# Moving work across the two joints of a batch in a software-pipelined transformer and expert kernel

## The reference

```python
xn = layernorm(x)                       # 16 x 512 x 128, f32
# branch 1
h = layernorm(xn) * g1 + b1
q, k, v = h@WQ+bQ, h@WK+bK, h@WV+bV     # 16 heads of 8
a = softmax(q k^T / sqrt(8), band: 0 <= i-j < 128)
attn_out = (a v) @ WO + bO
s_t = A * s_(t-1) + (h @ Bw)_t;  ssm_out = s @ Cw
g = sigmoid(h @ Wg + bg)
x1 = xn + g * attn_out + (1 - g) * ssm_out
h2 = layernorm(x1) * g2 + b2
S = x1 + gelu(h2 @ W1 + b1) @ W2 + b2   # the MLP, 128 -> 512 -> 128
# branch 2: 8 experts, top 2, in bf16 inputs
nf = rmsnorm(bf16(xn)) * nw;  w = softmax over the two largest of nf @ gate
out2 = bf16(xn) + sum over e of w_e * expert_e(nf)    # gated, clipped at 7
result = x + S * silu(out2)
```

## Time and profile before

| | |
|---|---|
| median of 3 runs | 1091.38 us (1089.91 to 1097.93) |
| profiled execution, its own time | 1094.57 us |
| its span | 1092.8 us |
| busy: TensorE, VectorE, ScalarE, GpSimd | 84%, 72%, 65%, 46% of the span |
| mean granted TensorE clock | 0.925 |
| DMA, mean | 69 GB/s |

### The profile page before, as it was taken

One profiled execution on the slowest core, in us unless ns is written; L12 is line 12 of the kernel. 1 busy time (PEld: TensorE's weight loads), 2 busy tenths in 40 slices (PEclk: granted clock), 3 DMA queues, 4 the chain that ended last, 5 costly groups with the idle time before them and its releaser, 6 DMA issues.

```text
span 1092.8 us, 38402 instructions
## 1 busy us (share of the span) xinstructions
PE 919.2 (84%) x15864; PEld 561.7 (51%) x15864; DVE 782.5 (72%) x1990; ACT 712.8 (65%) x1126; POOL 501.8 (46%) x786
## 2 busy tenths in 40 slices
PE   2567898989889898988889898989888898978877
PEld 1333564646455464645555464645555464635435
DVE  4476777887877677888777777887777788656216
ACT  3205685858677595858768595867768585746645
POOL 6226355372736356273626456273635547152331
PEclk7557999999999899999999999998999999978869
DMA  5552414123332404224241503223241402310000
GB/s 108 129 118 67 93 46 105 32 94 64 100 62 75 90 27 108 50 90 62 92 75 53 112 24 109 52 90 63 75 93 36 111 17 99 58 31 6 25 1 10
DMA packets 85599, 75.24 MB, mean 69 GB/s; under 512 B 9329, under 2 KB 79154, under 8 KB 85426
## 3 DMA queue, kind: packets, MB, share of 16 engines
q1 hardware_dynamic: 83346, 72.00, 28.3%
q10 hardware_dynamic: 2080, 0.79, 0.3%
HBM read 36.33 MB, written 30.15 MB: 61 GB/s over the span
## 4 chain that ended last, share of the span: by engine, by line
PE 48%; DVE 25%; issue 13%; ACT 9%; POOL 2%; DMA 2%; DVEq 0%; SPq 0%; POOLq 0%; ACTq 0%
PE ps L558 8%; DVE mx L1074 6%; PE ps L500 6%; PE ps L690 5%; PE ps L750 5%; PE ps L711 5%; ACT pt L831 4%; PE ps L489 3%; DVE gc L1131 3%; PE ps L570 2%; DVE lin L1124 2%; PE ps L575 2%; ACT ot L836 2%; DVE junk L950 2%; PE ps L684 2%
## 5 line engine op out<-in xcount | busy, mean ns | idle before, releaser
L831 ACT ACTIVATE pt<-ps 128x1024 f32<-128x1024 f32 (+1 forms) x256 | 234.7, 917 | 212.5 <-PE ps L489 211.1
L1074 DVE TENSOR_REDUCE mx<-ps 128x2 f32<-128x320 f32 (+1 forms) x512 | 230.9, 466 | 110.6 <-PE ps L515 107.6
L1253 POOL TENSOR_SCALAR_AFFINE_SELECT pt<-pt 128x512 f32<-128x512 f32 x256 | 170.7, 669 | 264.6 <-ACT pt L831 264.3
L500 PE MATMUL ps<-kd,qz 48*32 48x160 bf16 (+1 forms) x4096 | 160.5, 241 | 66.6 <-DVE mx L1074 34.2
L489 PE MATMUL ps<-qz,kd 51*32 51x256 bf16 (+1 forms) x4096 | 183.5, 272 | 6.1 <-ACT pt L831 3.8
L558 PE MATMUL ps<-pt,va 128*32 128x256 f32 (+1 forms) x2048 | 159.8, 397 | 33.2 <-ACT ot L836 33.0
L500 PEld LDWEIGHTS ps<-kd,qz 48*32 48x32 bf16 x4096 | 72.7, 91 | 218.7 <-issue 121.3
L690 PEld LDWEIGHTS ps<-m,act_t 128*128 128x128 f32 x1024 | 126.8, 191 | 53.6 <-DVE act_t L1152 38.6
L690 PE MATMUL ps<-m,act_t 128*128 128x128 f32 x1024 | 143.2, 283 | 11.6 <-DVE act_t L1152 11.6
L1256 POOL TENSOR_SCALAR_AFFINE_SELECT pt<-pt 128x512 f32<-128x512 f32 x192 | 124.6, 649 | 0.0
L879 ACT ACTIVATE lin<-ps,mbias 128x512 f32<-128x512 f32 x128 | 87.7, 685 | 48.7 <-DVE act_t L1152 29.5
(11 more groups left out here) (158 smaller groups left out, 1672.7 us busy)
## 6 DMA issues: line engine op xcount, KB each, us to landing
qz<-qk_parts SPq DMA_DIRECT2D x32, 384.0 KB, 7.3
kd<-qk_parts SPq DMA_DIRECT2D x32, 384.0 KB, 8.7
qk_parts<-qp SPq DMA_DIRECT2D x16, 384.0 KB, 2.4
qk_parts<-kp SPq DMA_DIRECT2D x16, 384.0 KB, 2.3
xl<-L_attn_x SPq DMA_DIRECT2D x16, 256.0 KB, 3.1
qk_parts<-qp SPq DMA_DIRECT2D x16, 256.0 KB, 2.9
qk_parts<-kp SPq DMA_DIRECT2D x16, 256.0 KB, 2.7
xnr<-xn SPq DMA_DIRECT2D x16, 256.0 KB, 3.3
```

What stands on the lines that cost most here:

```text
L500: nc.tensor.matmul(ps[QG * c:QG * (c + 1), 4 + par, w * pr:w * (pr + 1)], qz[q][rows, 2 * g + pr, P * i + QG * c:P * i + QG * (c + 1)], kd ...
L831: nc.scalar.activation(to, src, ACT.Exp, scale=SCALE).then_inc(exp_ok.sem, 1)
L1074: nc.vector.tensor_reduce(mx[:, i, HG * g + pr:HG * (g + 1):2], src, AX.X, ALU.max).then_inc(mx_ok.sem, 1)
L1253: sel1 = nc.gpsimd.affine_select(out=pt[:, s, :, 0:P], in_=pt[:, s, :, 0:P], compare_op=ALU.is_ge, fill=0.0, base=0, pattern=[[0, HG], [1, ...
```

## The change

- **Joint 1, TensorE and ScalarE.** `up(0)` with its share is issued in step 16, between the last values, and the two products of `up(1)` in step 17. The share product has a signal of its own (`share_ps`), and is waited for by VectorE's `gate`. ScalarE runs `lin(0)` and `ga(0)` before `aoT`. VectorE makes x1 during experts 1 (before: 0), its statistics during expert 2 (before: 1), and half of the statistics of batch b+3 during expert 0 (before: 2). h2 is made after expert 5 and transposed after `up(7)`.
- **Maxima.** `LEAD = 2`: the scores and maxima of steps 0 and 1 of batch b+2 are done at the end of body b (`first_scores`, `maxima`), and step n of the loop carries those of step n+2. The minus maxima are split and transposed in steps 14 and 15.
- **Joint 2.** The MLP's second product of batch b-1 is done in the next body, half in step 0 and half in step 1 (`mlp_down`); `sres` is made in step 2, the product with the states in step 1 (before: 0). `norm_h`, the two tanh and `finish` move into the steps. `norm_x` moves from ScalarE to VectorE, with four `tensor_scalar` (subtract, multiply) in place of four activations, and GpSimd no longer makes `b1n`. GpSimd's `ob` moves from step 2 to step 5.

The core of the diff:

```diff
-AT_STATES, AT_H0, AT_Q, AT_K, AT_U, AT_V, AT_G, AT_C = 0, 2, 4, 6, 8, 10, 12, 14
+LEAD = 2
+AT_STATES, AT_H0, AT_Q, AT_K, AT_U, AT_V, AT_G, AT_C = 1, 2, 4, 6, 8, 10, 12, 14
-AT_H2 = 4
-MIX = (9, 11, 15, 16)
+AT_H2 = 5
+MIX = (11, 13, 15, 16)
...
+            def maxima_free(b, n, half):
+                if n == 0 and half == 0:
+                    pe.wait_ge(*done(stacks_in, b))
+                    pe.wait_ge(*done(gc_ok, b - 2, E))
+                else:
+                    pe.wait_ge(*done(mx_ok, b, 2 * n - 1 + half))
+
+            def first_scores(b, q, n, half):
+
+                maxima_free(b, n, half)
+                for pr in range(2):
+                    score(b, q, n, half, pr)
+                score_mask(n, half)
...
+                def mlp_down(t):
+                    pe.wait_ge(*done(hid_ok, b - 1))
+                    for j in range(NJ):
+                        mm = nc.tensor.matmul(bank_t(6)[:, t], hid[:, j, P * t:P * (t + 1)], w2[:, j], start=j == 0, stop=j == NJ - 1)
+                    if t == NT - 1:
+                        mm.then_inc(w2_ps.sem, 1)
...
+                    if has(b - 1) and n < 2:
+                        mlp_down(2 * n)
+                        mlp_down(2 * n + 1)
...
+                    if main and n == NCH:
+                        up(0)
+                        share(0)
+                    if main and n == NCH + 1:
+                        up(1)
+                    if nxt and n == NCH - LEAD + 1:
+                        turn_shift()
...
-                    for t in range(NT):
-                        for j in range(NJ):
-                            if t == 0:
-                                pe.wait_ge(*done(hid_ok, b, j + 1))
-                            mm = nc.tensor.matmul(bank_t(6)[:, t], hid[:, j, P * t:P * (t + 1)], w2[:, j], start=j == 0, stop=j == NJ - 1)
-                    mm.then_inc(w2_ps.sem, 1)
...
+                    for n in range(LEAD):
+                        for half in range(2):
+                            first_scores(b + 2, q, n, half)
...
+            def norm_x(b, q, tiles):
+                if tiles[0] == 0:
+                    dve.wait_ge(*done(r1_step, b))
+                    dve.wait_ge(*done(xn_copied, b - 2))
+                for t in tiles:
+                    ts = nc.vector.tensor_scalar(xn[:, q, t], xl[:, q, t], mv[:, t, 0:1], r1[:, t:t + 1], ALU.subtract, ALU.mult)
+                ts.then_inc(xn_ok.sem, 1)
...
+                        if has(b - 1) and step == 5:
+                            dve.wait_ge(*done(w2_ps, b - 1))
+                            dve.wait_ge(*done(x1b_ok, b - 1))
+                            dve.wait_ge(*done(ob_ok, b - 2))
+                            nc.vector.tensor_tensor(sres[:], bank_t(6), x1b[:], ALU.add).then_inc(s_ok.sem, 1)
+                        if has(b - 1) and step in (7, 9):
+                            finish(b - 1, (step - 7) // 2)
...
-                        if e == 0:
+                        if e == 1:
                             dve.wait_ge(*done(wo_ps, b))
...
-                    if n == 2 and has(b - 1):
+                    if n == 5 and has(b - 1):
                         pool.wait_ge(*done(w_ok, b - 1))
```

More of the change, by code:

```diff
@@ L671, in up @@
                     if e == 0:
+                        pe.wait_ge(*done(nfT_ok, b))
                         pe.wait_ge(*done(exp_ok, b))
@@ new lines, in body @@
+                if main:
+                    turn_out(b, NG - 1)
+                    for t in range(NT):
+                        mm = nc.tensor.matmul(bank_t(6)[:, t], st[:, b % 3, P * t:P * (t + 1)], ncw[:], start=t == 0, stop=False,
+                                              skip_group_check=True)
+                    mm.then_inc(ncw_ps.sem, 1)
+                    pe.wait_ge(*done(ao_ok, b, NG))
+                    turn4(bank(7), lambda t: ao[:, t]).then_inc(aoT_ps.sem, 1)
+                    share(1)
@@ L836, in body @@
                         nc.scalar.activation(ot[:], bank(6), ACT.Copy).then_inc(ot_ok.sem, 1)
+                    if nx2 and n < 2:
+                        norm_h(2 * n)
+                        norm_h(2 * n + 1)
+                    if has(b - 1) and n == 2:
+                        soft_gate()
+                    if nxt and n == 3:
+                        mix_gate()
+                    if nxt and n == NCH - LEAD + 1:
+                        act.wait_ge(*done(nm_ps, b + 1))
+                        act.wait_ge(*done(shift_in, b))
+                        nc.scalar.activation(nmT[:], bank_bf(5)[0:NPART * H, :], ACT.Copy).then_inc(nmT_ok.sem, 1)
                     if nx2:
@@ L888, in body @@
                                 nc.scalar.activation(h2[:, t], x1[:, t], ACT.Identity, bias=b3n[:, t:t + 1], scale=r3[:, t:t + 1]).then_inc(h2_ok.sem, 1)
-                        if e == E - 1 and nx3:
-                            for t in range(NT):
-                                norm_x(t)
                         if e == 6:
@@ L905, in body @@
                     nfn_in()
-                if nx3:
-                    if not main:
-                        for t in range(NT):
-                            norm_x(t)
-                    for t in range(NT):
-                        norm_h(t)
             schedule(act, body)
@@ L1185, in body @@
                     nc.vector.tensor_tensor(z[:], xcr[:], cb[:], ALU.add).then_inc(z_ok.sem, 1)
-                if main:
-                    dve.wait_ge(*done(w2_ps, b))
-                    dve.wait_ge(*done(x1b_ok, b))
-                    dve.wait_ge(*done(ob_ok, b - 1))
-                    nc.vector.tensor_tensor(sres[:], bank_t(6), x1b[:], ALU.add).then_inc(s_ok.sem, 1)
+                if nx2:
+                    if start(b, -2):
+                        dve.wait_ge(masks_set.sem, N_MASKS)
+                        route_rank(0)
+                    for n in range(LEAD):
+                        for pr in range(2):
+                            maxima(b + 2, n, pr)
             set_spare(dve, "dve_waited")
```

216 lines of the change are left out of this document (100 added, 116 removed).

## The result

The changed kernel takes **1142.88 us** (median of 4 runs, 1138.9 to 1153.1), the kernel before 1093.97 beside it: a ratio of 1.0462, 95% interval 1.038 to 1.0544. The profiled execution spans 1137.1 us against 1092.8. So it is slower by 49 us, where 20 were forecast, and outside the range. The medians here take all runs of a kernel; a ratio leaves out the runs that lie over 1.5% above that kernel's fastest.

The account below looks back on a forecast made before the run. It took TensorE as leading, at VectorE's pace in the later steps. Joint 1 (16 times, -23), joint 2 (14 times, +45) and prologue (-2) gave +20 us, so 1111 us; range 1080 to 1130.

Parts of the forecast that it names:

- End of the values: Joint 1: two `up`, a share and the minus maxima ahead of the last values make their end 1.2 us later.
- Joint 1 worth -1.45 a batch: Joint 1: values' end 1.2 us later, gate of expert 1 gaining 2.65, net -1.45 us, 16 times.
- the 0.6: From joint 1: VectorE 0.8 us later at gate 4, of which 0.6 delays the last `down`, counted at joint 2.
- Joint 2, +3.2 a batch: Last `down` to VectorE's run from `qr`: the run starts 3.1 us later, taken as 3.2, 14 times.
- rival A: Faster: TensorE's 4.8 us of waits in the steps absorb the product, joint 2 at 0, so 1066 us; chance 0.14.
- 2.95 come back as a wait and as scores: Ahead of step 0: of the 3.74 us the product leaves, 2.95 return as wait and scores, 0.8 are won.
- rival C: Much slower: TensorE's clock falls more often at both joints, 1125 to 1140 us; chance 0.12.
- The wait of `values(0)` for `sres`, 0.9: Step 3, joint 2: TensorE's `values(0)` stands about 0.9 us for `sres`, queued on VectorE behind maxima and `s1`.
- `xn` on VectorE, 0.25 each and hidden: Joint 2: four `norm_x` steps on VectorE, 1.0 us in all, hidden by its 1.34 us wait for `cb`.
- `ob` in step 5, "0, at most 0.5": GpSimd's `ob` ahead of `qp`'s split, where GpSimd has gaps: costs 0, at most 0.5 us.
- Rival B: No difference: GpSimd and VectorE collide less, nf shortens, 14 to 28 us in all, about 1091 us; chance 0.22.
- Prologue -2: Prologue: the first exponential no longer waits for `h0`, -2 us (bounds -5 and +3).

Follow-up runs that it names:

- j1_only: The kernel before with joint 1 of the change alone (first experts' products among the last values); 1091.21 us, ratio 0.9998.
- j2_only: The changed kernel with joint 1's orders as in the kernel before, so joint 2's part alone; 1148.79 us, ratio 1.0526.
- l0_fill_steps: The changed kernel with lead 0, `states` in step 0 and joint 1's products in TensorE's waits, MLP's second product still in steps 0 and 1; 1070.16 us, ratio 0.9788.
- lead0: The changed kernel with `LEAD` 0 instead of 2, the product still in steps 0 and 1; 1094.79 us, ratio 1.0037.
- states0: The changed kernel with the states' part in step 0, so `s1` comes a step earlier; 1135.17 us, ratio 1.0389.
- best_ob_mix: best_ob with the routing's half steps of the kernel before (9, 11, 15, 16); 1048.34 us, ratio 0.9606.
- best_ob: l0_fill_steps with GpSimd's `ob` in step 12 instead of step 5; 1055.77 us, ratio 0.9674.
- fill_lead2: l0_fill_steps with a lead of 2 again; 1128.8 us, ratio 1.0335.
- ob_late: The changed kernel with GpSimd's `ob` in step 12 instead of step 5; 1141.94 us, ratio 1.0469.

## Why the prediction was wrong, point by point

- **Gate of expert 1, 4.8 us behind the values: right** (4.7). End of the values 1.2 later: 1.06 in the mean, but by luck. At full clock it is 1.64, and the clock, which before fell there in 5 of 13 batches, in after fell in none.
- **Joint 1 worth -1.45 a batch: too much.** With the 0.6 that the prediction books at joint 2 its own net is 1.2 - 2.65 + 0.6 = -0.85. j1_only, at full clock, shows 1.39 - 1.42, nothing: the gate comes 2.7 us earlier, but `cb` only 1.42; I let 0.6 be lost behind the gate, and 1.3 were. After itself shows -2.14 to `cb`, close to my -2.05 by luck. The other 0.7 needs joint 2's part (in j2_only it is 0.43), whose four `xn` left ScalarE. I had put that at nothing, "since ScalarE's saving isn't on the path at this place". The rows of before, just ahead of the earlier trace rows, speak against it: ScalarE runs from the `xn` into `cb` with no wait. That the `xn` are the cause is read from them; no run moved the `xn` alone.

```profile
575.62 1.64 ACT L789 ACTIVATE xn<-xl,b1n,r 128x128 f32<-128x128 f32 x4
577.27 1.28 ACT L900 ACT_TABLE_LOAD   x1
578.57 2.42 ACT L900 ACTIVATE hid<-ps,b1c 128x512 f32<-128x512 f32 x4
```

- **Joint 2, +3.2 a batch: the sum came out, its cause did not.** Without the 0.6 the prediction has 14.4 us from the last `down` to step 5, against 592.31 - 580.40 = 11.91 before. The joint shown above, at full clock, has 624.35 - 610.02 = 14.33: 2.62 up to step 0 where I had 2.35, 11.71 from there where I had 12.06. The step that failed is the conclusion from it, that the 3.74 us of the product "left a joint where TensorE had no gap for a stretch where it had almost none either". The way from the last `down` to step 5 holds the product in either order, so moving it costs nothing: l0_fill_steps has it in the steps and reaches `qp` no later than before, so joint 2 has the price that **rival A** gave it, 0. What costs is the term that I passed over, "2.95 come back as a wait and as scores": the lead. From l0_fill_steps to after, `cb` to `qp` grows by 15.50 - 11.68 = 3.82: late `s1` 0.92 (lead0 against l0_fill_steps), the lead 2.90 (lead0 against after).
- **The lead's 2.90 in two parts.** In the joint shown above `cb` to `qp` is 624.86 - 610.13 = 14.73, 2.13 more than lead0's 12.60: the scores ahead go in turn with VectorE's maxima while nothing else is ready. In the joint a batch earlier the same stretch takes 1.54 more, by the clock alone:

TensorE's product and ScalarE's marks there:

```profile
548.04 3.37 PE L596 MATMUL ps<-w,hid 128*128 128x128 f32 x16
...
544.66 0.60 ACT L931 ACTIVATE cb<-ps 128x512 bf16<-128x512 f32 x1 [0.20 <-PE ps L673]
...
560.93 0.68 ACT L836 ACTIVATE qp<-ps,bQ 128x512 bf16<-128x512 f32 x1
```

Windows of both joints (length, busy times; third column from the right: granted clock):

```profile
544.00:548.04 4.04, 2.57 (x94) 1.50 (x92) 3.30 (x10) 2.55 (x4) 0.00 (x0) 0.92 0.15 50
548.04:551.41 3.37, 3.37 (x29) 3.25 (x32) 0.64 (x2) 1.60 (x3) 1.22 (x2) 0.58 0.22 64
...
609.25:613.29 4.04, 2.57 (x96) 1.64 (x95) 3.33 (x11) 2.76 (x4) 0.00 (x0) 1.00 0.13 36
613.29:615.34 2.05, 2.05 (x32) 1.93 (x32) 0.74 (x2) 1.60 (x3) 0.83 (x2) 1.00 0.42 121
```

  Half the product takes 3.37 us at 0.58 and 2.05 at 1.00, behind the same 4.04 us with the same busy 2.57. It happens in 7 of after's 14 joints, every other one: 7 x 1.54 = 11 us. So the clock of **rival C** was at work at joint 2, for a quarter of the lead's loss. As a difference between the two kernels it comes to little: at the end of the values, where C's own row stands, before loses 0.6 us a batch to the clock and after nothing. At full clock throughout, after's batch is still 3.1 us longer. That the measured time lies just above C's 1125 to 1140 says nothing for C.
- **The wait ahead of step 0, "about 1 us": right** (1.11, then 0.36). **The wait of `values(0)` for `sres`, 0.9: wrong in place.** `turn_h0`, queued ahead of it, waits 1.03 for `s1`, which the change had put a step later; I had read the table of steps and not asked who needs `s1`. That the two waits are near in size is luck. Only where that wait is gone (states0) does `sres` show, with 0.47.
- **`xn` on VectorE, 0.25 each and hidden: right.** Four take 1.11 us, in the wait for `cb`, of which 0.31 is left.
- **`ob` in step 5, "0, at most 0.5": wrong.** This is the term put at nothing that weighs most. It stands beside VectorE's squares. Their mean before, after, and in best_ob_mix:

```profile
L950 DVE CUSTOM_DVE_ANT_0 junk<-xc 128x128 bf16<-128x128 bf16 x64 | 29.3, 493 | 0.0
```

```profile
L989 DVE CUSTOM_DVE_ANT_0 junk<-xc 128x128 bf16<-128x128 bf16 x64 | 39.9, 659 | 0.0
```

```profile
L989 DVE CUSTOM_DVE_ANT_0 junk<-xc 128x128 bf16<-128x128 bf16 x64 | 30.0, 505 | 0.0
```

  With the rest of VectorE's run it makes `kp` to `ot` 0.8 longer (of the 0.97 in the table), worth 14 us from l0_fill_steps to best_ob. Rival B's collisions are real, but the change made more of them, not fewer.
- **Prologue -2: wrong, about +6** (first `aoT` 126.7 before, 132.8 after); 5 of it is the late `states` (states0).

In sum: the batch came out 3.11 longer and not 1.75. Of the 1.36 between them joint 2 is +0.85 (3.45 for 2.6; 0.77 of it the clock), the stretch with `ob` +0.97, another stage -0.21, the end of the values -0.14 and `aoT` to `cb` -0.09, these two small by luck; the prologue comes on top with 8. So in the number what failed is mostly `ob` put at nothing (14 us), the clock at joint 2 left out of the forecast (11) and the prologue (8). The sum for joint 2 was sound and its reading was not: it blamed the product, and the lead was at fault.

## What to carry to other kernels

A wait on the critical path is filled with work that is ready, and nothing else: joint 1's products were worth nothing ahead of the last values and 10 us in the waits behind them. Work that two engines do in turn (a score, its maximum, the next score) should not be pulled into a place where neither has anything else; leave it where long work of a third kind stands between its halves. And price an edit of several parts by its parts: here one constant, the lead, cost 48 to 59 us and hid that the product's place in the steps was worth 20 to 30 beside the other moves. Before blaming a moved piece, ask whether the stretch that you compare holds it in both orders. And before reading the mean of a stage, separate the batches in which the clock fell.

## What the runs showed of the hardware

**The same joint loses the clock in one batch and keeps it in another.** With the lead and the product in the steps, 14 joints of a kernel have scores ahead. In after the granted clock falls in every other one (7), in fill_lead2 in all 14, in states0 in 12, in ob_late in 6, in j2_only in 2. All 14 of each have the same pair of waits, 1.11 and 0.36 us, and the same 4 us of 2.6 busy ahead of the product. In lead0, l0_fill_steps and best_ob_mix, which have no such pair, the product never falls below full speed. So an edit that removes a wait can be paid back by the clock: states0 took 0.55 us out of a joint with the lower clock (`cb` to `qp` 15.72 against 16.27) and had nearly all its joints there; ob_late took 0.83 out of the steps and lost it at the end of the values. The product of one joint of fill_lead2:

```profile
604.72 3.17 PE L596 MATMUL ps<-w,hid 128*128 128x128 f32 x16
607.68 1.61 PE L632 MATMUL ps<-cw,st 128*128 128x128 f32 x8
```

against 2.05 and 1.06 at full clock. The Trainium skill (TensorE: Matmul & The Clock Gate, HAM oscillation) tells of a loop in which a long wait for data brings the clock down in every turn, so that the next work runs slower. The trace agrees in that the next work pays (3.17 us for 2.05); here the waits are short, and not every turn is hit. Why the same joint is hit in one batch and spared in the next was not tried and stays open.

**GpSimd beside VectorE.** Moving one 128x512 addition of GpSimd away from the four squares (128x128, bf16) brings them from 644 (l0_fill_steps) to 567 ns (best_ob), while `nf`, nearer to its new place, goes from 671 to 734; with the routing's pieces moved too they are 505 and 687. The Trainium skill (SBUF — State Buffer, the section on SBUF's two separate sides) says that the two share a pair of ports which one holds for a whole instruction. The durations of single squares fit: with no instruction of GpSimd beside them they take 273 to 283 ns in every trace, beside `ob` and a mask 705 to 1017 in after. Which part of the hardware they meet at no run shows.
